# Attention on VectorE: both row statistics in the sixth step and the row moments in the eighth

## The chip, the cores and the metric

The kernel runs on one core of a Trainium2 chip. The metric is the time of one execution on the device in microseconds (us), smaller is better. Five engines work side by side from queues of their own: TensorE (PE, its weight loads are shown as PEld), VectorE (DVE), ScalarE (ACT), GpSimd (POOL) and SyncE (SP, which here only issues DMAs). They meet through semaphores alone. A name with a q behind it (DVEq, SPq) is the engine's own instruction queue.

## The reference, cut to what matters

An input of 32 x 375 x 256 is tokenised by a convolution of stride 2 to B = 32 batches of S = 188 rows of D = 256 columns, then comes an attention with 16 heads of 16 columns, then a mixture of 16 experts. The change lies in the attention stage and in what that stage prepares for the next layer norm.

```python
h = _L0_tok_ref(x, ...)
h = h + _L0_attn_ref(_layernorm(h, axis=-1), ...)
h = h + _L0_ffn_ref(_layernorm(h, axis=-1), ...)

# _L0_attn_ref
scores = jnp.einsum('bhqd,bhkd->bhqk', qh, k_rec) / math.sqrt(d)
scores = scores * decay[None, None, :, :]
attn = jax.nn.softmax(scores, axis=-1)
out = jnp.einsum('bhqk,bhkd->bhqd', attn, v_rec)
return out.transpose(0, 2, 1, 3).reshape(b, s, d) @ W_o

# _layernorm
m = jnp.mean(x, axis=axis, keepdims=True)
v = jnp.var(x, axis=axis, keepdims=True)
```

The mean and the variance of each row of h after the attention are what "row statistics" and "row moments" mean below: `bn_stats` makes six numbers of a row of 256, `bn_aggr` makes mean and variance of the six.

## The kernel before

The attention stage is a software pipeline written out by hand. Every engine runs its own function `batch(b, par)` for b from -3 to 33, in the same order, b = 2 to 27 of them in a loop whose body holds two batches (the even one, then the odd one), the others as straight code. A batch has eight steps, j = 0 to 7, one for each pair of heads. "Step 5" below is the step with j = 5, which is the sixth.

In a step PE makes the scores of a pair of heads that lies LEAD = 11 steps ahead (`scores`, L1395, into the banks `SB`), subtracts the row maxima from the previous step's turned scores (`take_max`, L1409), makes the turned scores of this step (`turned_scores`, L1420, into `TB`), in odd steps weighs the values (`weigh`, L1441), and then does one job of another batch: in step 0 it projects values (L1463), in step 1 it turns the normalised rows (L1482), in step 2 it makes the output projection of batch b - 2 (L1498), in steps 4 and 6 it projects queries and keys of batch b + 3 (L1452), in step 5 it turns the maxima (L1508).

DVE's two fixed tasks of a step are `row_max` (three custom instructions of line L1086, each with a read of its accumulator) and `times_decay` (L1094). They and PE form a tight loop:

- `scores` of a step waits for `row_max` of the step before (semaphore `scaled`), and `row_max` waits for the step's `scores`;
- `times_decay` of step j waits for `turned_scores` of step j, and `take_max` of step j, which PE does in its step j + 1, waits for `times_decay` (semaphore `multiplied`).

The queue of DVE is in order, so whatever stands between two `row_max` delays both. The other tasks of DVE stand behind `times_decay` of their step:

- `x_norm` (L1036, step 0) normalises the rows of batch b + 3;
- `add_out` (L1059) and `invert` (L1052), step 3, for batches b - 2 and b - 1: `invert` makes the reciprocals of the softmax sums;
- `row_stats` (L1065), `row_moments` (L1072), `keep_moments` (L1078), for batch b - 2. Each waits on `dve2` or `y_added` for what it reads. `keep_moments` copies the moments of `row_moments` to `MV`, and waits for them. Nothing reads `MV` of these batches before the attention stage has ended;
- `low_max` (L1044, step 6), for which PE's `weigh` of step 7 waits.

A second chain goes round through the other engines, and the change doesn't touch any instruction of it. SP's order in a batch is a fixed list of 24 or so DMA issues: the spread queries and keys of later batches (L456), the reciprocals to memory (L485, waits for `invert`), more keys (L456), the store of the queries' halves (L462), the reciprocals back as rows (L496), and the store of the keys' halves (L462, waits for POOL's low halves of the keys, L592). When the reciprocals have landed, POOL multiplies by them (`divide`, L614), makes the high half (L618) and, at the start of its next batch, the low half (L592). The output projection of batch b - 2 on PE in step 2 (L1498) waits for that low half (`otl_ready`):

```python
                    pe.wait_ge(otl_ready, b - 1)
```

Of the kernel before, what the change touches and what calls it, by code (L numbers as in the profile page):

```python
# [105 lines left out]
def build(nc, x_t, conv_w, conv_b, gamma, beta, wq, wk_t, wv_t, wo, w_down, w_up_k, w_up_v, gate, s_g, s_u, s_d,  # L106
# [7 lines left out]
    with ctx:  # L114
# [167 lines left out]
        def valid(b):  # L282

            return not isinstance(b, int) or 0 <= b < B
# [119 lines left out]
        def hold(eng):  # L404

            eng.sem_inc(passed, 1)
# [537 lines left out]
        def _(dve):  # L944
# [83 lines left out]
            def x_norm(c):  # L1028
                if not valid(c):
                    return  # L1030
                if not isinstance(c, int) or c >= 1:
                    dve.wait_ge(xt_done, c)
                hold(dve)
                for qt in range(2):
                    t = 2 * c + qt
                    last = nc.vector.tensor_scalar(XN[0:HT, qt * D:(qt + 1) * D], H[0:HT, t, :], MV[0:HT, t, 0:1],  # L1036
                                                   RSTD[0:HT, t, :], ALU.subtract, ALU.mult)
                last.then_inc(xn_ready, 1)

            def low_max(c, par):  # L1040
                if valid(c):
                    dve.wait_ge(mth_ready, 2 * c + 2)
                    for p in (0, 32):
                        last = nc.vector.scalar_tensor_tensor(MT[par][64 + p:64 + p + HP, :], MB[p:p + HP, 0:S], -1.0 / 16, MT[par][p:p + HP, :],  # L1044
                                                              ALU.mult, ALU.subtract)
                    last.then_inc(mt_ready, 1)

            def invert(c):
                if valid(c):
                    dve.wait_ge(sums_in, 16 * c + 16)  # L1050
                    at_least(dve, rs_out, 16 * c)
                    nc.vector.reciprocal(RS[0:64, :], SUMS[0:64, :]).then_inc(sums_inverse, 1)  # L1052

            def add_out(c):
                if valid(c):
                    dve.wait_ge(y_done, c + 1)
                    hold(dve)
                    both = H[0:HT, bass.ts(c, 2), :].rearrange("p t n -> p (t n)")
                    nc.vector.scalar_tensor_tensor(both, WB[0:HT, :], 1.0 / WSCALE, both, ALU.mult, ALU.add).then_inc(y_added, 1)  # L1059

            def row_stats(c, qt):
                if valid(c):
                    dve.wait_ge(y_added, c + 1)
                    hold(dve)
                    nc.vector.bn_stats(STAT2[qt][0:HT, :], H[0:HT, 2 * c + qt, :]).then_inc(dve2, 1)  # L1065

            def row_moments(c):
                if valid(c):
                    dve.wait_ge(dve2, 5 * c + 2)
                    hold(dve)  # L1070
                    for qt in range(2):
                        nc.vector.bn_aggr(AGGR2[0:HT, 2 * qt:2 * qt + 2], STAT2[qt][0:HT, :]).then_inc(dve2, 1)  # L1072

            def keep_moments(c):
                if valid(c):
                    dve.wait_ge(dve2, 5 * c + 4)
                    hold(dve)
                    nc.vector.tensor_copy(MV[0:HT, bass.ts(c, 2), :], hsplit(AGGR2[0:HT, :])).then_inc(dve2, 1)  # L1078

            def row_max(b, par, j):  # L1080
                c, cpar, i = ahead(b, par, j, LEAD)
                if valid(c):
                    dve.wait_ge(s_done, HP * c + i + 1)
                    hold(dve)
                    for t in range(3):
                        last = nc.vector.tensor_tensor_reduce(  # L1086
                            out=SC[t], in0=SB[t], in1=C[:, C_DECAY + t * S:C_DECAY + (t + 1) * S], scale=1.0, scalar=-3e38,
                            op0=ALU.mult, op1=ALU.max, accum_out=MAX[cpar][:, t * HP + i:t * HP + i + 1])
                    last.then_inc(scaled, 1)

            def times_decay(b, j):
                if valid(b):
                    dve.wait_ge(st_done, HP * b + j + 1)
                    nc.vector.tensor_tensor(TB[j % 2], TB[j % 2], C[:, C_DECAY:C_DECAY + 3 * S], ALU.mult).then_inc(multiplied, 1)  # L1094

            def batch(b, par):
                for j in range(HP):
                    row_max(b, par, j)
                    times_decay(b, j)
                    if j == 0:  # L1100
                        x_norm(b + 3)
                    elif j == 3:
                        add_out(b - 2)
                        invert(b - 1)
                    elif j == 4:
                        row_stats(b - 2, 0)
                    elif j == 5:
                        row_stats(b - 2, 1)
                    elif j == 6:
                        low_max(b + 1, 1 - par)  # L1110
                        row_moments(b - 2)
                    elif j == 7:
                        keep_moments(b - 2)

            batches(dve, batch)
            meet(dve)

# [648 lines left out]
```

## Time and profile before

| | |
|---|---|
| time before, median of 3 runs (lowest to highest) | 1870.95 us (1870.95 to 1874.34) |
| time of the profiled execution | 1870.4 us |
| its span, first to last instruction | 1868.6 us |
| attention stage | from about 150 us to 794 us of the span |
| a batch of the loop, undisturbed | 18.03 us (for one: DVE's L1094 of step 0 at 450.88 and at 468.91) |
| PE busy over the span | 1689.0 us, 90% |
| DVE busy over the span | 1224.8 us, 66% |
| POOL busy over the span | 950.2 us, 51% |

The profiled execution lies 1.8 us over its span, so what changes in the span changes in the time by as much. The columns of a timeline row are its start in us from the start of the span, its length in us, the engine, the source line, the operation, what it writes and reads, and in square brackets how long its engine stood idle before it and what ended the idle time. Rows of matmuls are merged, and their ends are modelled.

### The profile page before, as it was taken

The numbers are of one execution on the slowest core, as the hardware profiler recorded it, in microseconds if no ns is written. First come the engines' busy times: TensorE is split into PE (matmuls) and PEld (weight loads), VectorE is DVE, ScalarE is ACT, GpSimd is POOL, SyncE is SP. The second block draws the span as 40 slices with busy tenths as digits, with TensorE's granted clock in tenths as the row PEclk, the third lists the DMA queues.
The fourth block names the chain that finished last, engine by engine and source line by source line (L and its number), as shares of the span: only waits on it lengthen the run. The fifth ranks groups of instructions, "written<-read, shape, count | busy, mean of one in ns | idle before, by whom it ended". The sixth has DMA issues, their size and how long they took to land.

```text
span 1868.6 us, 46715 instructions
## 1 busy us (share of the span) xinstructions
PE 1689.0 (90%) x15566; PEld 1232.2 (66%) x15566; DVE 1224.8 (66%) x3739; ACT 902.6 (48%) x1965; POOL 950.2 (51%) x945
## 2 busy tenths in 40 slices
PE   6874899999999999579999669999999999999997
PEld 5873566666666665357777537777777777777775
DVE  3883788888888888384778655555555555555551
ACT  4442566666666665244233634444444444444442
POOL 3771244444444443272224054666666666666665
PEclk9995999999999999789999779999999999999999
DMA  5522455555555555242010232333333334333322
GB/s 189 176 94 50 106 121 126 134 123 133 132 127 128 129 136 116 50 133 51 26 34 26 96 123 86 102 101 97 93 93 100 98 100 101 101 101 99 101 34 28
DMA packets 220234, 186.52 MB, mean 100 GB/s; under 512 B 165625, under 2 KB 200953, under 8 KB 214009
## 3 DMA queue, kind: packets, MB, share of 16 engines
q1 hardware_dynamic: 193272, 141.11, 28.2%
q0 software_dynamic: 26880, 44.36, 11.5%
q8 instruction: 48, 0.79, 0.2%
q14 instruction: 34, 0.27, 0.0%
HBM read 134.49 MB, written 50.44 MB: 99 GB/s over the span
## 4 chain that ended last, share of the span: by engine, by line
PE 70%; DVE 12%; issue 8%; POOL 4%; SPq 2%; ACT 2%; DMA 2%; DVEq 1%; POOLq 0%; ACTq 0%
PE psum L1678 26%; PE psum L1695 13%; PE psum L1542 6%; PE psum L1560 4%; DVE arena L1086 4%; DVE psum L1094 3%; PE psum L1441 3%; PE psum L1498 2%; PE psum L1395 2%; PE psum L1409 2%; PE psum L1463 2%; PE psum L1420 2%; POOL hidden L570 2%; POOL arena L575 1%; PE psum L1508 1%
## 5 line engine op out<-in xcount | busy, mean ns | idle before, releaser
L1678 PE MATMUL psum<-arena,hidden 128*128 128x376 f16 x3072 | 493.1, 323 | 0.9 <-DVE arena L1320 0.9
L634 POOL TENSOR_TENSOR arena<-arena 128x376 f16<-128x376 f32 x320 | 317.4, 994 | 343.9 <-ACT arena L727 342.5
L1678 PEld LDWEIGHTS psum<-arena,hidden 128*128 128x128 f16 x3072 | 301.0, 98 | 188.9 <-issue 1.6
L727 ACT ACTIVATE arena<-arena 128x376 f16<-128x376 f32 (+5 forms) x610 | 287.3, 474 | 54.0 <-DVE arena L1250 43.1
L1086 DVE CUSTOM_DVE_ANT_0 arena<-psum,constants 128x188 f32<-128x188 f32 x768 | 228.0, 345 | 106.8 <-PE psum L1395 105.4
L727 ACT ACTIVATE arena<-psum 128x188 f32<-128x188 f32 (+7 forms) x457 | 168.1, 398 | 257.6 <-PE psum L1658 74.9
L926 ACT ACTIVATE arena<-psum 128x376 f32<-128x376 f32 x256 | 123.7, 483 | 342.2 <-PE psum L1678 342.2
L1330 DVE SCALAR_TENSOR_TENSOR arena<-psum,arena 128x376 f32<-128x376 f32 x256 | 140.8, 550 | 189.3 <-ACT arena L926 187.8
L1695 PE MATMUL psum<-hidden,arena 128*128 128x256 f16 (+1 forms) x2304 | 256.6, 273 | 0.0
L1695 PEld LDWEIGHTS psum<-hidden,arena 128*128 128x128 f16 (+1 forms) x2304 | 229.8, 103 | 21.8
L776 ACT ACTIVATE arena<-psum 128x564 f32<-128x564 f32 x256 | 164.0, 641 | 98.6 <-PE psum L1409 97.0
L1312 DVE SCALAR_TENSOR_TENSOR hidden<-arena,hidden 128x512 f16<-128x512 f32 x192 | 209.2, 1095 | 0.0
L592 POOL TENSOR_TENSOR arena<-arena 128x376 f16<-128x376 f32 x128 | 115.5, 902 | 171.9 <-ACT arena L727 166.0
L1094 DVE TENSOR_TENSOR psum<-psum,constants 128x564 f32<-128x564 f32 x256 | 191.1, 747 | 7.4 <-PE psum L1420 7.2
L679 POOL DMA_INDIRECT out<-hidden,arena x96 | 149.8, 1561 | 45.2 <-DVE hidden L1340 23.1
L1340 DVE TENSOR_SCALAR hidden<-psum,arena 128x256 f32<-128x256 f32 x96 | 46.3, 483 | 164.9 <-PE psum L1695 164.6
L1542 PE MATMUL psum<-arena,weights_hi 128*128 128x376 f16 x512 | 136.3, 327 | 1.2 <-DVE arena L1125 1.2
L1441 PE MATMUL psum<-arena 128*32 128x188 f32 (+1 forms) x2048 | 126.7, 336 | 4.6 <-ACT arena L776 0.8
L1409 PE MATMUL psum<-arena 128*128 128x188 f16 x768 | 106.3, 247 | 26.4 <-DVE psum L1094 20.4
L1395 PE MATMUL psum<-arena 96*128 96x188 f16 x768 | 108.6, 251 | 23.0 <-DVE arena L1086 13.2
L670 POOL DMA_INDIRECT arena<-token_table,arena x96 | 109.8, 1144 | 26.9 <-POOL arena L663 12.7
L727 ACT ACTIVATE hidden<-arena 128x512 f16<-128x512 f32 x192 | 117.9, 619 | 0.0
(156 smaller groups left out, 2644.2 us busy)
## 6 DMA issues: line engine op xcount, KB each, us to landing
arena<-q_halves SPq DMA_DIRECT2D x384, 47.0 KB, 2.4
arena<-k_halves SPq DMA_DIRECT2D x384, 47.0 KB, 2.3
arena<-e_g SPq DMA_DIRECT2D x16, 1024.0 KB, 5.1
arena<-e_u SPq DMA_DIRECT2D x16, 1024.0 KB, 5.2
arena<-e_d SPq DMA_DIRECT2D x16, 1024.0 KB
arena<-x_t SPq DMA_DIRECT2D x32, 376.0 KB, 3.5
weighed<-arena POOLq DMA_DIRECT2D x32, 376.0 KB, 3.9
q_halves<-arena SPq DMA_DIRECT2D x32, 188.0 KB, 3.1
```

The lines of the kernel that those rows point to most:

```text
L634: nc.gpsimd.tensor_tensor(dst, f, hi, ALU.subtract).then_inc(ready, 1)
L679: nc.gpsimd.indirect_dma_start(out[:, :], bass.IndirectOffsetOnAxis(ap=IDXS[par][0:n, m:m + 1], axis=0), EO[par][0:n, m * D:(m + 1) * D], ...
L727: return nc.scalar.activation(dst, src, ACT.Copy, scale=scale)
L776: nc.scalar.activation(PT[i % RING], TB[i % 2], ACT.Exp).then_inc(exp_done, 1)
L1086: last = nc.vector.tensor_tensor_reduce(out=SC[t], in0=SB[t], in1=C[:, C_DECAY + t * S:C_DECAY + (t + 1) * S], scale=1.0, scalar=-3e38, op ...
L1094: nc.vector.tensor_tensor(TB[j % 2], TB[j % 2], C[:, C_DECAY:C_DECAY + 3 * S], ALU.mult).then_inc(multiplied, 1)
L1312: nc.vector.scalar_tensor_tensor(WEL[par][:, c], WST[:, c], WSCALE, WEH[par][:, c], ALU.mult, ALU.subtract).then_inc(wl_ready[i], 1)
L1395: last = mm(SB[t], QD[cpar][0:2 * KR, i * CW + t * 128:i * CW + (t + 1) * 128], KX[cpar][0:2 * KR, i * S:(i + 1) * S], start=True, stop=True)
L1441: last = mm(OB[32 * k:32 * k + 32, :], V[cpar][p0:p0 + rows, v:v + 32], PT[a % RING][p0:p0 + rows, t * S:(t + 1) * S], start=n == 0, stop= ...
L1542: last = mm(bank[2 * (m % 2) + i][:, 0:CHUNK], w_, a, start=n == 0, stop=n == 5)
L1678: last = mm(bank[2 * (s % 2) + i][:, 0:CHUNK], w_, a, start=n == 0, stop=n == 5)
L1695: last = mm(bank[down_bank[m]][0:rows, 0:D], a, w_, start=n == 0, stop=n == 23)
```

## The change

Both `row_stats` calls of a batch move into step 5, behind its `times_decay`; before, one stood in step 4 and one in step 5. `row_moments` moves from step 6, where it stood behind `low_max`, to step 7, behind `times_decay` and directly ahead of `keep_moments`. `add_out` and `invert` stay in step 3. No instruction is added or taken away.

```diff
                     elif j == 3:
                         add_out(b - 2)
                         invert(b - 1)
-                    elif j == 4:
+                    elif j == 5:
                         row_stats(b - 2, 0)
-                    elif j == 5:
                         row_stats(b - 2, 1)
                     elif j == 6:
                         low_max(b + 1, 1 - par)
+                    elif j == 7:
                         row_moments(b - 2)
-                    elif j == 7:
                         keep_moments(b - 2)
```

In DVE's queue, in the even batch of the loop, the end of step 6 and the start of step 7 read before (L1044 is `low_max`, L1072 `row_moments`, L1086 the first instruction of `row_max` of step 7; ISA and REGISTER_ALU rows are semaphore and address work of the queue):

```order
L1044 SCALAR_TENSOR_TENSOR arena<-psum,arena 8x188
L1069 ISA
L1072 BN_AGGR arena<-arena 94x2 [waits dve2]
L1072 BN_AGGR arena<-arena 94x2
L1083 REGISTER_ALU
L1086 ISA arena<-psum,constants 128x188 [waits scores_done]
```

The end of step 7 and the start of step 0 of the next batch read before (L1094 is `times_decay` of step 7, L1078 `keep_moments`, L1086 `row_max` of step 0):

```order
L1093 REGISTER_ALU
L1094 TENSOR_TENSOR psum<-psum,constants 128x564 [waits turned_scores_done]
L1076 REGISTER_ALU
L1078 ISA [waits dve2]
L1078 COPY mean_var<-arena 94x4
L1083 REGISTER_ALU
L1086 ISA arena<-psum,constants 128x188 [waits scores_done]
```

The same place of the changed kernel, with the same names:

```order
L1093 REGISTER_ALU
L1094 TENSOR_TENSOR psum<-psum,constants 128x564 [waits turned_scores_done]
L1069 ISA
L1072 BN_AGGR arena<-arena 94x2 [waits dve2]
L1072 BN_AGGR arena<-arena 94x2
L1076 REGISTER_ALU
L1078 ISA [waits dve2]
L1078 COPY mean_var<-arena 94x4
L1083 REGISTER_ALU
L1086 ISA arena<-psum,constants 128x188 [waits scores_done]
```

The two aggregations have moved past a whole `row_max` and `times_decay`, and the copy, which waits for them, is now their direct neighbour in the queue.

In step 5 of the changed kernel DVE's queue reads, from `times_decay` of step 5 to `row_max` of step 6:

```order
L1094 TENSOR_TENSOR psum<-psum,constants 128x564 [waits turned_scores_done]
L1065 BN_STATS arena<-hidden 94x6 [waits y_added]
L1065 ISA [waits y_added]
L1065 BN_STATS arena<-hidden 94x6
L1083 REGISTER_ALU
L1086 ISA arena<-psum,constants 128x188 [waits scores_done]
```

The first L1065 stood one `row_max` and one `times_decay` further ahead before. The queues of ACT and SP and the work of PE and POOL are the same in both kernels.

## Rows read from the trace of the kernel before

**Rows 1.** First line of the page.

```profile
span 1868.6 us, 46715 instructions
```

**Rows 2.** Timeline of DVE, step 6 of batch 14 to step 1 of batch 15.

```profile
466.24 0.24 DVE L1072 BATCH_NORM_AGGREGATE arena<-arena 94x2 f32<-94x6 f32 x2
466.51 0.35 DVE L1086 CUSTOM_DVE_ANT_0 arena<-psum,constants 128x188 f32<-128x188 f32 x1
...
467.34 0.75 DVE L1094 TENSOR_TENSOR psum<-psum,constants 128x564 f32<-128x564 f32 x1
468.00 0.16 DVE L1078 COPY mean_var<-arena 94x4 f32 x1
468.09 0.35 DVE L1086 CUSTOM_DVE_ANT_0 arena<-psum,constants 128x188 f32<-128x188 f32 x1
...
468.91 0.75 DVE L1094 TENSOR_TENSOR psum<-psum,constants 128x564 f32<-128x564 f32 x1
469.57 0.72 DVE L1036 TENSOR_SCALAR arena<-hidden,mean_var,rstd 94x256 f32 x2
470.78 0.35 DVE L1086 CUSTOM_DVE_ANT_0 arena<-psum,constants 128x188 f32<-128x188 f32 x1 [0.49 <-PE psum L1395]
...
471.61 0.75 DVE L1094 TENSOR_TENSOR psum<-psum,constants 128x564 f32<-128x564 f32 x1
```

**Rows 3.** Timeline of PE, steps 0 and 2 of batch 15.

```profile
467.48 0.42 PE L1395 MATMUL psum<-arena 96*128 96x188 f16 x3 [0.19 <-DVE arena L1086]
468.15 0.42 PE L1409 MATMUL psum<-arena 128*128 128x188 f16 x3 [0.25 <-DVE psum L1094]
...
472.54 0.41 PE L1409 MATMUL psum<-arena 128*128 128x188 f16 x3
...
473.03 0.42 PE L1498 MATMUL psum<-weights_hi,arena 128*94 128x256 f16 x2
```

**Rows 4.** Timeline of DVE, end of step 5 and start of step 6, batch 14.

```profile
462.61 0.41 DVE L1065 BATCH_NORM_STATS2 arena<-hidden 94x6 f32 x1
463.89 0.35 DVE L1086 CUSTOM_DVE_ANT_0 arena<-psum,constants 128x188 f32<-128x188 f32 x1 [0.88 <-PE psum L1395]
```

**Rows 5.** Timeline of DVE in the convolution: a copy that waits for L970.

```profile
107.53 0.27 DVE L1000 COPY mean_var<-arena 94x8 f32 x1 [0.24 <-DVE arena L970]
```

**Rows 6.** Timeline of POOL, batch 15: divide, then low half.

```profile
470.19 0.99 POOL L614 TENSOR_TENSOR arena<-arena 128x376 f32<-128x376 f32 x1 [2.18 <-DMA arena<-inverse_sums]
...
471.95 0.90 POOL L592 TENSOR_TENSOR arena<-arena 128x376 f16<-128x376 f32 x1
```

**Rows 7.** Timeline, batches 7 and 27: low half and output projection.

```profile
327.20 0.90 POOL L592 TENSOR_TENSOR arena<-arena 128x376 f16<-128x376 f32 x1
...
328.25 0.41 PE L1498 MATMUL psum<-weights_hi,arena 128*94 128x256 f16 x2
...
688.97 0.90 POOL L592 TENSOR_TENSOR arena<-arena 128x376 f16<-128x376 f32 x1
...
690.09 0.42 PE L1498 MATMUL psum<-weights_hi,arena 128*94 128x256 f16 x2
```

**Rows 8.** Timeline of POOL and SP, end of batch 13.

```profile
449.07 0.90 POOL L592 TENSOR_TENSOR arena<-arena 128x376 f16<-128x376 f32 x1 [3.51 <-ACT arena L727]
...
450.13 0.41 SPq L462 DMA_DIRECT2D k_halves<-arena  x1
```

**Rows 9.** Timeline of DVE and POOL, step 0 of batch 14.

```profile
451.25 0.98 POOL L614 TENSOR_TENSOR arena<-arena 128x376 f32<-128x376 f32 x1 [1.28 <-DMA arena<-inverse_sums]
...
451.54 1.17 DVE L1036 TENSOR_SCALAR arena<-hidden,mean_var,rstd 94x256 f32 x2
```

**Rows 10.** Timeline of DVE and POOL, step 0 of batch 27.

```profile
686.63 0.72 DVE L1036 TENSOR_SCALAR arena<-hidden,mean_var,rstd 94x256 f32 x2
687.19 1.02 POOL L614 TENSOR_TENSOR arena<-arena 128x376 f32<-128x376 f32 x1 [2.13 <-DMA arena<-inverse_sums]
```

**Rows 11.** Timeline of POOL and DVE, step 7 of batch 30.

```profile
756.65 0.97 POOL L614 TENSOR_TENSOR arena<-arena 128x376 f32<-128x376 f32 x1 [6.59 <-DMA arena<-inverse_sums]
756.72 0.94 DVE L1078 COPY mean_var<-arena 94x4 f32<-94x4 f32 x1
```

## The prediction

> **What bounds the kernel now.** The change touches the attention stage alone, which is about a third of the span [rows 1], so I read DVE's timeline there first. The steady batches are alike to 0.01 us, and I take batch 15 as the example.
>
> In step 7 and step 0 DVE is never idle, and PE waits for it. The aggregations start at 466.24 and `row_max` of step 7 at 466.51; `times_decay` of step 7 starts at 467.34 and ends at 468.09, and PE's `take_max` starts at 468.15 after 0.25 us of idleness, as its `scores` did at 467.48 after 0.19 [rows 2, 3]. So 0.27 us of `row_moments` lie on the path between PE and DVE there. In step 1 it is the other way round: DVE idles 0.49 us until PE's scores are there [rows 2].
>
> Then I asked who else holds PE in a batch, and read POOL beside PE. In batch 15 POOL's low half of the attention output starts at 471.95, ends at 472.85, and PE's output projection, which waits for it, starts at 473.03, 0.18 later [rows 3, 6]. In batch 7 the distance is 328.25 - 328.10 = 0.15, in batch 27 it is 690.09 - 689.87 = 0.22; [rows 7]; these are the first and the last of the eleven odd batches 7 to 27, over which it is 0.14 to 0.22. The shortest, 0.14, must be what the release of PE takes. So in every second batch PE comes to its output projection less than 0.1 us after the half is there, and in six of the eleven exactly when it is: **two paths end together**.
>
> Where does that half come from? From the reciprocals' DMA, for which `divide` waited 2.18 us [rows 6]; that DMA is late because SP issues it as the last but one of its list, and SP began the list when the keys' halves of batch 13 were there: POOL's L592 at 449.07 to 449.97, SP's store at 450.13 [rows 8]. From there to `divide` are 470.19 - 450.13 = 20.06 us. The store is released by PE's key projection in step 6 of batch 13. So the loop is closed over two batches: key projection of batch 13, POOL, SP's list, DMA, `divide`, output projection in step 2 of batch 15, four steps of PE, key projection of batch 15. None of the moved instructions lies on it: steps 2 to 6 hold only the statistics, which I cost below at nothing. **This loop sets the pace of two batches; the path through step 7 and step 0 is as long as it to within 0.1 us.**
>
> **The change part by part.**
>
> *The first `row_stats` leaves step 4.* It frees 0.33 us on DVE ahead of `row_max` of step 5. PE doesn't wait for DVE in step 5 or at the start of 6: it weighs, turns the maxima, and then DVE waits for PE, 0.88 us [rows 4]. Gain 0. If PE did wait, 0.33 a batch.
>
> *It arrives in step 5*, where two statistics now end about 0.33 us later than the one did, inside those 0.88 us [rows 4]. Cost 0; without that cover 0.33 a batch, about 10 us in all.
>
> *`row_moments` leaves step 6.* `row_max` and `times_decay` of step 7 start 466.51 - 466.24 = 0.27 us sooner [rows 2], and with them `take_max` in PE's step 0. This is -0.27 a batch for the path of PE and DVE.
>
> *It arrives in step 7, with a copy right behind that waits for it.* Behind `times_decay` now come 0.24 us of aggregations, then the copy's own wait. The trace has that wait in the convolution, where a copy with address work in its queue stands 0.24 us idle behind the same operation [rows 5]. Before, the copy's moments were a step old and the copy started on the tick at 468.00 [rows 2]. The bounds are nothing and 0.24; I take 0.24, it is the same pair of operations. From `times_decay` of step 7 now starting at 467.07: aggregations at 467.73 to 467.97, copy at 468.21, `row_max` of step 0 at 468.3 to 468.4 instead of 468.09. So DVE is 0.2 to 0.3 us later in step 0 than before, while PE is 0.27 earlier. What hides it: PE doesn't need step 0 of DVE until `take_max` of step 1, behind the value projection, and in step 1 DVE had 0.49 us to spare [rows 2]. After: `times_decay` of step 0 at about 469.15, `x_norm` 469.8 to 470.55, scores there at 470.5. So the -0.27 survives to PE's step 1. If that cover were gone the step would be 0.25 a batch slower.
>
> The Trainium skill has a rule on this term: on the page "VectorE: DVE Perf Modes", section "The DRAIN you can't avoid", chained operations with a semaphore after each took as long as without, "the semaphore costs nothing extra here". By it the copy would start at 467.97 and DVE would be level with before. The trace doesn't agree, by 0.24 us [rows 5], and the sum goes by the trace; either way the sum is the same, since step 1 hides it.
>
> *`x_norm` against `divide`.* In even batches `divide` (451.25 to 452.23) lies on `x_norm`, which takes 1.17 instead of 0.72 us and ends 0.48 after it [rows 9]. There `x_norm` ends with `divide`, so a later start costs nothing, and PE, which has 0.12 us to spare behind `times_decay` of step 1 (472.54 against 472.36 + 0.06 [rows 2, 3]), gets at first only some 0.1 of its 0.27 us. As even batches get earlier, their `divide` does too.
>
> *What reaches the end.* In an odd batch PE arrives early at its output projection and waits for POOL. Of -0.27 a batch only the excess over 0.14 us is left: 0.01, 0, 0.04, 0, 0.04, 0, 0, 0, 0.08, 0, 0.08, together **0.25 us** for the eleven odd batches. Outside this regime a boundary between batches counts in full, if nothing else holds PE. I count one on the way in (batch 4 to 5) and two on the way out (27 to 28 and 29 to 30), 3 x 0.24 = **0.7 us** as an estimate from the 0.27. The boundary 30 to 31 gives nothing: the copy stands under `divide` there, 0.94 us long [rows 11], and will again. The last two batches have no `row_max`, and the chain of the reciprocals sets them.
>
> Sum: 0.25 + 0.7 = 0.95, so the profiled execution's 1870.4 becomes about 1869.5. The median of the runs is 0.55 above it, so I say 1870.0.
>
> **The rivals.**
>
> *The whole gain arrives (faster).* If PE's odd output projection isn't held by POOL, or POOL's chain gets shorter with PE, each of the 29 boundaries of batches 2 to 30 gives 0.27: 7.8 us, 1863. For it: PE's idle time is real [rows 3] and goes away. Against it: eleven times a distance within 0.08 us of the shortest isn't chance. Chance 0.12.
>
> *`divide` catches `x_norm` in odd batches too (slower).* Its two instructions, of 0.40 us each, take 0.72 together, so they start 0.32 us apart, and the second is caught if `divide` starts before it. `divide` starts 0.62 us behind `x_norm` in batch 15 and 0.56 in batch 27, the smallest; the largest is 1.00 [rows 2, 6, 10]. The margin is thus 0.24 to 0.68 us. A DVE that is 0.2 to 0.3 later in step 0 uses up the smallest, if the even batch gave nothing back; if it gave 0.27 back, as I expect once the pattern has settled, `x_norm` starts where it did. Price of a catch: `x_norm` ends at 471.18 + 0.47 = 471.65, `take_max` of step 1 can start at 473.29 instead of 472.54, so 0.75 us for an odd batch. Five catches are 3.7 us and eleven 8.3; the point from which it decides is a shift of some 0.3 us. I put it at +5, 1876. The Trainium skill, "SBUF — State Buffer", section "SBUF: two separate sides", says that VectorE and GpSimd take a shared port in turn for a whole instruction, "the other fully blocks"; the trace agrees, with 1.17 us and 0.94 us [rows 9, 11]. Chance 0.08.
>
> *The same, but by drift.* DMAs land at other times and the loop over two batches takes 0.1 us more or less each time; 11 x 0.2 = 2.2 us either way. This is inside the forecast.
>
> **How the numbers follow.** A measurement of this kernel can tell about 0.2%, 3.7 us, from no change. No change that shows: 0.80, faster 0.12, slower 0.08. The likeliest case has its own range 1867 to 1874 (the sum, the drift of 2.2, and the highest of the runs shown, 1874.34). With the outer cases let in by half the range is 1864 to 1875.
>
> **What would show it.** In the changed profile, from `times_decay` of step 7 to that of step 0 about 2.1 us instead of 468.91 - 467.34 = 1.57, and `row_max` of step 7 right behind `low_max`, where L1072 stood; a copy with about 0.24 us of idle time behind L1072; PE waiting for POOL's L592 ahead of L1498 in all odd batches by 0.2 to 0.5 us; two batches still 36.1 us. Wrong would be: two batches at 35.6 or less (the first rival), or `x_norm` above 1 us in odd batches (the second). What I can't see is whether the wait of the copy also holds the queue's later address work, so that DVE falls back further than 0.3 us.

## The result, and the profile after

The changed kernel takes 1877.02 us (median of 22 runs, 1872.74 to 1882.10) against 1873.89 us before (22 runs, 1870.95 to 1879.71): 3.1 us more. The ratio is 1.0019 with a 95% interval of 1.0012 to 1.0027. I had forecast no change at 1870.0 us. Of the 7.0 us between that and the result 2.9 are the median of the kernel before, which was 1870.95 over the three runs shown and 1873.89 over 22; 3.1 are the kernel; the rest is the 0.95 us of gain that I had summed up and that did not come.

The profiled execution has a span of 1872.7 us against 1868.6 [rows 1]. Head of its page:

```profile
span 1872.7 us, 46715 instructions
PE 1690.0 (90%) x15566; PEld 1230.2 (66%) x15566; DVE 1235.2 (66%) x3739; ACT 904.4 (48%) x1965; POOL 946.8 (51%) x945
```

The same number of instructions, and DVE is busy 10.4 us longer (1235.2 against 1224.8). Most of it has nothing to do with the change: 6.6 us belong to the 192 instructions of one line of the experts' stage (L1312 before, L1311 now, 210.1 against 216.8 us). The two instructions of `x_norm` (L1036) take 34.5 us in all instead of 32.4. The sum hides what matters below: over the batches 8 to 27, `x_norm` became shorter in the even batches (1.26 to 0.85 us on average) and longer in the odd ones (0.72 to 1.22 us).

As a measure that the scatter of single runs at the start and the end of the stage doesn't touch, I use the time of two batches, from the start of DVE's `times_decay` in step 0 of batch 8 to that in step 0 of batch 28, divided by ten. Before: (704.01 - 342.16) / 10 = 36.18 us. After: (709.83 - 343.58) / 10 = 36.63 us. That is 0.44 us for two batches, 5.7 us if all thirteen pairs of the loop lose as much. From batch 28 to batch 31 the changed kernel was 1.5 us faster (704.01 to 757.57 before and 709.83 to 761.84 now), but over the traces of this document this stretch takes anything from 52.0 to 56.9 us, so that is not shown to be an effect of the change. The measure comes from one trace of each kernel. The kernel before, the same without `x_norm` and the one with the statistics alone give 36.18, 36.18 and 36.30 us below, so differences of about 0.1 us mean nothing.

First the boundary between steps 7 and 0 in DVE's timeline, at the end of batch 13, which is the last batch of the loop's body (it answers to [rows 2]):

```profile
451.30 0.75 DVE L1094 TENSOR_TENSOR psum<-psum,constants 128x564 f32<-128x564 f32 x1
451.95 0.23 DVE L1072 BATCH_NORM_AGGREGATE arena<-arena 94x2 f32<-94x6 f32 x2
452.44 0.17 DVE L1078 COPY mean_var<-arena 94x4 f32 x1 [0.26 <-DVE arena L1072]
453.10 0.35 DVE L1086 CUSTOM_DVE_ANT_0 arena<-psum,constants 128x188 f32<-128x188 f32 x1 [0.49 <-issue]
...
453.93 0.75 DVE L1094 TENSOR_TENSOR psum<-psum,constants 128x564 f32<-128x564 f32 x1
```

and at the end of batch 14, in the middle of the loop's body:

```profile
469.42 0.75 DVE L1094 TENSOR_TENSOR psum<-psum,constants 128x564 f32<-128x564 f32 x1
470.08 0.23 DVE L1072 BATCH_NORM_AGGREGATE arena<-arena 94x2 f32<-94x6 f32 x2
470.56 0.17 DVE L1078 COPY mean_var<-arena 94x4 f32 x1 [0.25 <-DVE arena L1072]
470.82 0.35 DVE L1086 CUSTOM_DVE_ANT_0 arena<-psum,constants 128x188 f32<-128x188 f32 x1
...
471.65 0.75 DVE L1094 TENSOR_TENSOR psum<-psum,constants 128x564 f32<-128x564 f32 x1
```

The copy waits 0.25 us for its neighbours in both, as forecast. But then `row_max` of step 0 doesn't follow it in 0.09 us as before. At the end of batch 14 it starts 0.26 us behind the copy's start, at the end of batch 13 it starts 0.66 us behind, of which 0.49 are idle time that no other engine causes. From `times_decay` of step 7 to that of step 0 these are 2.23 and 2.63 us, where it was 1.57 in every batch; the two lengths alternate through the whole loop. The trace's records of the queue itself show what stands in the longer one: behind the copy, the compare and branch of the loop (L299) and a register instruction of the same line.

The last batches are straight code, without a branch and without addresses to work out. There the same place, at the end of batch 28, reads:

```profile
725.56 0.75 DVE L1094 TENSOR_TENSOR psum<-psum,constants 128x564 f32<-128x564 f32 x1
726.22 0.23 DVE L1072 BATCH_NORM_AGGREGATE arena<-arena 94x2 f32<-94x6 f32 x2
726.60 0.17 DVE L1078 COPY mean_var<-arena 94x4 f32<-94x4 f32 x1
726.78 0.35 DVE L1086 CUSTOM_DVE_ANT_0 arena<-psum,constants 128x188 f32<-128x188 f32 x1
727.61 0.75 DVE L1094 TENSOR_TENSOR psum<-psum,constants 128x564 f32<-128x564 f32 x1
```

The copy follows the aggregations after about 0.15 us instead of 0.25, `row_max` follows the copy after 0.18, and from `times_decay` to `times_decay` it is 2.05 us. So the neighbourhood alone costs 0.48 us (2.05 instead of 1.57), the address work 0.18 more, and the branch 0.40 more.

What that does in step 1 of the even batch, in PE's timeline (`take_max` in PE's steps 0 and 1, and the output projection, now L1497; it answers to [rows 3]):

```profile
452.10 0.42 PE L1408 MATMUL psum<-arena 128*128 128x188 f16 x3 [0.23 <-DVE psum L1094]
...
454.74 0.42 PE L1408 MATMUL psum<-arena 128*128 128x188 f16 x3 [0.20 <-DVE psum L1094]
...
457.35 0.42 PE L1497 MATMUL psum<-weights_hi,arena 128*94 128x256 f16 x2
```

The second wait, of PE for `times_decay` of step 0, did not exist before; it stands in each of the even batches 8 to 26. And in an odd batch, here batch 17, DVE first and then POOL and PE:

```profile
508.19 0.75 DVE L1094 TENSOR_TENSOR psum<-psum,constants 128x564 f32<-128x564 f32 x1
508.85 1.54 DVE L1036 TENSOR_SCALAR arena<-hidden,mean_var,rstd 94x256 f32 x2
510.31 0.34 DVE L1086 CUSTOM_DVE_ANT_0 arena<-psum,constants 128x188 f32<-128x188 f32 x1
...
509.24 1.00 POOL L614 TENSOR_TENSOR arena<-arena 128x376 f32<-128x376 f32 x1 [2.34 <-DMA arena<-inverse_sums]
...
511.26 0.42 PE L1394 MATMUL psum<-arena 96*128 96x188 f16 x3 [0.18 <-DVE arena L1086]
511.93 0.41 PE L1408 MATMUL psum<-arena 128*128 128x188 f16 x3 [0.25 <-DVE psum L1094]
```

`divide` started 0.39 us behind `x_norm` instead of 0.56 or more, and `x_norm` took 1.54 us instead of 0.72. `row_max` of step 1 followed at once, and PE waited for both tasks of it. Of the ten odd batches 9 to 27 seven have such an `x_norm`, of 1.36 to 1.54 us, and in all seven PE waits for `times_decay` of step 1. In five of them `divide` starts behind `x_norm`, in two (11 and 21) up to 0.10 us ahead of it. The other three (9, 15, 23) have `x_norm` at 0.72 us and wait for POOL's low half, 0.43 to 0.95 us. In batch 15 `divide` was just too late to stretch `x_norm`, and became longer itself:

```profile
472.31 0.72 DVE L1036 TENSOR_SCALAR arena<-hidden,mean_var,rstd 94x256 f32 x2
472.72 1.17 POOL L614 TENSOR_TENSOR arena<-arena 128x376 f32<-128x376 f32 x1 [2.36 <-DMA arena<-inverse_sums]
```

Measured on PE, from `turned_scores` of step 0 to that of the next batch, an even batch takes 18.22 us on average instead of 18.03, and an odd one 18.44 instead of 18.15.

Step 5 is as forecast (it answers to [rows 4]):

```profile
464.73 0.74 DVE L1065 BATCH_NORM_STATS2 arena<-hidden 94x6 f32 x2
466.25 0.35 DVE L1086 CUSTOM_DVE_ANT_0 arena<-psum,constants 128x188 f32<-128x188 f32 x1 [0.79 <-PE psum L1394]
```

DVE still waits 0.79 us for PE behind the two statistics.

### The profile page after: what moved, and what is told of

Its sections match the earlier page's. It is cut to its first block, busy times and chain, and to the rows that moved or that the text cites. A ratio compares the mean times of both kernels' runs of the same rounds, so it can differ in the third digit from the quotient of the medians.

```text
span 1872.7 us, 46715 instructions
## 1 busy us (share of the span) xinstructions
PE 1690.0 (90%) x15566; PEld 1230.2 (66%) x15566; DVE 1235.2 (66%) x3739; ACT 904.4 (48%) x1965; POOL 946.8 (51%) x945
## 4 chain that ended last, share of the span: by engine, by line
PE 63%; DVE 12%; issue 9%; POOL 6%; SPq 3%; DMA 3%; ACT 2%; DVEq 1%; POOLq 0%; ACTq 0%
PE psum L1677 26%; PE psum L1694 13%; PE psum L1541 6%; DVE arena L1086 4%; PE psum L1559 4%; DVE psum L1094 4%; SPq L456 2%; PE psum L1497 2%; PE psum L1440 2%; POOL hidden L570 2%; PE psum L1408 1%; POOL arena L575 1%; PE psum L1394 1%; DMA arena<-inverse_sums 1%; PE psum L1657 1%
## 5 line engine op out<-in xcount | busy, mean ns | idle before, releaser
L1086 DVE CUSTOM_DVE_ANT_0 arena<-psum,constants 128x188 f32<-128x188 f32 x768 | 228.4, 346 | 101.7 <-PE psum L1394 93.0
L1311 DVE SCALAR_TENSOR_TENSOR hidden<-arena,hidden 128x512 f16<-128x512 f32 x192 | 215.9, 1129 | 0.0
L592 POOL TENSOR_TENSOR arena<-arena 128x376 f16<-128x376 f32 x128 | 115.2, 900 | 180.4 <-ACT arena L727 175.0
L1094 DVE TENSOR_TENSOR psum<-psum,constants 128x564 f32<-128x564 f32 x256 | 191.2, 747 | 7.0 <-PE psum L1419 6.8
```

What stands on the lines that cost most here:

```text
L1086: last = nc.vector.tensor_tensor_reduce(out=SC[t], in0=SB[t], in1=C[:, C_DECAY + t * S:C_DECAY + (t + 1) * S], scale=1.0, scalar=-3e38, op ...
L1311: nc.vector.scalar_tensor_tensor(WEL[par][:, c], WST[:, c], WSCALE, WEH[par][:, c], ALU.mult, ALU.subtract).then_inc(wl_ready[i], 1)
```

## The experiments

My theory after the result, A, says that the loss is the wait of the copy for its direct neighbours in DVE's queue. It costs its own 0.25 us and also uncovers what the queue would else have done under running work: the work on addresses (0.17 us more) and at the end of the loop's body the branch (another 0.4). DVE is then 0.4 and 0.8 us behind in step 0, which is more than the room that it had there. The rivals: B, the second statistic in step 5; C, the loop's branch alone; D, the place of the aggregations in step 7 as such; and, from the prediction, whether POOL's chain really is a second path of the same length.

Each ratio is taken against runs of the kernel before that were made together with those of the row.

| kernel | two batches, us | start of step 0's L1094 (L1095), batch 8, batch 28 | ratio to before, 95% interval |
|---|---|---|---|
| before | 36.18 | 342.16, 704.01 | |
| after | 36.63 | 343.58, 709.83 | 1.0019 (1.0012 to 1.0027) |
| statistics alone | 36.30 | 343.79, 706.82 | 1.0003 (0.9991 to 1.0016) |
| aggregations alone | 36.82 | 346.71, 714.95 | 1.0025 (1.0014 to 1.0036) |
| aggregations moved in even batches | 36.54 | 340.31, 705.75 | 1.0012 (1.0000 to 1.0024) |
| aggregations moved in odd batches | 36.52 | 348.45, 713.63 | 1.0015 (1.0004 to 1.0026) |
| aggregations ahead of step 7's `times_decay` | 36.10 | 343.41, 704.37 | 0.9988 (0.9976 to 1.0000) |
| aggregations and copy in step 5 | 35.90 | 340.83, 699.86 | 0.9977 (0.9967 to 0.9987) |
| the same, both statistics in step 4 | 35.84 | 341.59, 700.01 | 0.9975 (0.9963 to 0.9986) |
| after, no `x_norm` in the loop | 36.06 | 342.39, 702.96 | one run |
| before, no `x_norm` in the loop | 36.18 | 342.22, 704.04 | one run |
| before, chain longer | 37.11 | 344.47, 715.55 | 1.0058 (1.0041 to 1.0074) |
| after, chain longer | 37.01 | 344.21, 714.31 | 1.0051 (1.0033 to 1.0069) |
| statistics in 4, rest in 5, chain longer | 36.76 | 343.64, 711.20 | 1.0057 (1.0040 to 1.0073) |

**The statistics alone.**

```diff
-                    elif j == 4:
-                        row_stats(b - 2, 0)
                     elif j == 5:
+                        row_stats(b - 2, 0)
                         row_stats(b - 2, 1)
```

> Only the two statistics are moved to step 5; the aggregations stay in step 6. Theory A (the copy's own wait behind the aggregations in step 7 costs the time): no change, ratio 1.000 within 0.001, two batches of the loop 36.1 to 36.3 us as before, from times_decay of step 4 to that of step 5 about 1.57 us and from step 5 to step 6 about 3.0. Theory B (the second statistic in step 5 comes too late for step 6): as slow as the full change, 36.6 us for two batches.

Measured: 36.30 us, 1.0003. From `times_decay` of step 4 to step 5 it is 1.56 to 1.57 us in every batch, and 3.0 from step 5 to step 6. The 0.12 us above the kernel before are within what single traces differ by. B falls: the statistics cost nothing that can be measured.

**The aggregations alone.**

```diff
                         low_max(b + 1, 1 - par)
-                        row_moments(b - 2)
                     elif j == 7:
+                        row_moments(b - 2)
                         keep_moments(b - 2)
```

> Only the aggregations are moved, to step 7; the statistics stay in steps 4 and 5. Theory A: the whole loss, ratio 1.0015 to 1.003, two batches 36.6 us, from times_decay of step 7 to that of step 0 2.23 us after an even batch and 2.64 after an odd one. Theory B: as before, 36.2 us.

Measured: 36.82 us, 1.0025: the whole loss, with 2.23 and 2.63 us from step 7 to step 0. It is 0.2 us above the changed kernel in this one trace. There in four even batches (8, 12, 18 and 26) `x_norm` takes 1.62 to 1.69 us although `divide` had ended by then: it runs together with the two operations that follow on POOL, the high half (L618) and the low half (L592).

**In even batches or in odd batches alone.** The kernel for even batches; the other has the two conditions exchanged. Both have the statistics in step 5.

```diff
                     elif j == 6:
                         low_max(b + 1, 1 - par)
+                        if par == 1:
+                            row_moments(b - 2)
                     elif j == 7:
+                        if par == 0:
+                            row_moments(b - 2)
                         keep_moments(b - 2)
```

> Both statistics in step 5; the aggregations move to step 7 in even batches alone, so that their copy's wait never stands ahead of the loop's branch. Theory A: 2.23 us from step 7 to step 0 after even batches, 1.57 after odd ones; the odd batch's x_norm is 0.4 us later and meets the divide, while even batches are as before: two batches 36.2 to 36.5 us, ratio 1.000 to 1.0015. If the branch alone mattered (theory C), it would be at or below before, 36.1.

> The aggregations move to step 7 in odd batches alone, the last of the loop's body. Theory A: 2.64 us from step 7 to step 0 after odd batches, PE waits 0.2 us for times_decay in step 1 of even batches, which gain nothing or lose 0.1 to 0.2 us; odd batches as before, held by POOL's chain: two batches 36.2 to 36.4 us. Theory C (the exposed branch is the whole loss): 36.6 us, ratio 1.002.

Measured: 36.54 and 36.52 us, both slower, both with the boundaries as expected (2.23 and 1.57; 1.57 and 2.63). C falls in its strong form, since the kernel without any uncovered branch is slower too, by 0.36 us for two batches; its ratio alone, 1.0012 with an interval down to 1.0000, would not say it clearly. Both lie above what I expected of A (36.2 to 36.5 and 36.2 to 36.4), and the second taken by itself fits C better. Each half alone costs more than half, so the two effects don't add up. A doesn't explain this: in the kernel for even batches six of the ten odd batches (9, 11, 15, 17, 19, 21) have `x_norm` at 0.72 us, and PE waits 0.42 to 1.48 us for POOL there. From the end of SP's last read issue to `divide` it is 3.13 us on average instead of 2.87. Why the reads land later was not settled. In the kernel for even batches the copy of batch 14, which waits for its neighbours, and that of batch 15, whose aggregations are a step old, stand in DVE's timeline like this:

```profile
467.90 0.17 DVE L1078 COPY mean_var<-arena 94x4 f32 x1 [0.25 <-DVE arena L1072]
468.16 0.35 DVE L1086 CUSTOM_DVE_ANT_0 arena<-psum,constants 128x188 f32<-128x188 f32 x1
...
485.99 0.15 DVE L1078 COPY mean_var<-arena 94x4 f32 x1
486.08 0.35 DVE L1086 CUSTOM_DVE_ANT_0 arena<-psum,constants 128x188 f32<-128x188 f32 x1
```

The second is at the loop's branch, and yet `row_max` follows in 0.09 us: the branch costs nothing where the queue has run ahead.

**The aggregations ahead of `times_decay` in step 7.** All else as in the changed kernel.

```diff
                     row_max(b, par, j)
+                    if j == 7:
+                        row_moments(b - 2)
                     times_decay(b, j)
...
                     elif j == 7:
-                        row_moments(b - 2)
                         keep_moments(b - 2)
```

> As the full change, but the aggregations of step 7 stand ahead of that step's times_decay instead of behind it, so that 0.65 us of other work lie between them and the copy that waits for them. Theory A (the wait of a neighbour, which also holds the queue's later work, is the loss): back to before, from times_decay of step 7 to that of step 0 1.57 us, two batches 36.1 to 36.3 us, ratio 1.000. Theory D (any place of the aggregations in step 7 is too late for step 0): 36.6 us, ratio 1.002.

Measured: 36.10 us, 0.9988, with 1.53 us from step 7 to step 0 behind even batches and 1.82 behind odd ones, where I expected 1.57 behind both. The loss is gone with the neighbourhood; D falls. At the end of batch 15, the last of the loop's body, DVE's timeline is:

```profile
486.09 0.72 DVE L1094 TENSOR_TENSOR psum<-psum,constants 128x564 f32<-128x564 f32 x1
486.73 0.16 DVE L1078 COPY mean_var<-arena 94x4 f32 x1
487.09 0.35 DVE L1086 CUSTOM_DVE_ANT_0 arena<-psum,constants 128x188 f32<-128x188 f32 x1 [0.20 <-issue]
```

The copy starts without idle time. The branch shows a little, 0.20 us: the copy's wait is over only 0.1 us behind the start of `times_decay`, and the queue reaches the branch 0.4 us behind it. In the kernel before, the branch was done before `times_decay` of step 7 started.

**Aggregations and copy in step 5**, where VectorE stood idle 0.88 us [rows 4]; in the second kernel both statistics stand in step 4.

```diff
                     elif j == 5:
                         row_stats(b - 2, 1)
+                        row_moments(b - 2)
+                        keep_moments(b - 2)
                     elif j == 6:
                         low_max(b + 1, 1 - par)
-                        row_moments(b - 2)
-                    elif j == 7:
-                        keep_moments(b - 2)
```

> Statistics in steps 4 and 5 as before, and the aggregations and the copy right behind them in step 5, where VectorE was idle 0.88 us. Steps 6 and 7 lose the 0.27 us of the aggregations and the 0.09 of the copy. The copy's wait is the same as in the changed kernel, but under cover. Theory A with two paths of one length (POOL's chain holds every odd batch): two batches 36.0 to 36.2 us, ratio 0.999 to 1.000, PE waits for POOL ahead of the output projection in all odd batches. Rival (no chain): 0.3 us less for each batch, 35.5 us for two, ratio 0.995.

> Both statistics in step 4, aggregations and copy in step 5: as the kernel with all in step 5, but with 0.33 us more of cover in step 5 and 0.33 us less in step 4. Theory A with two paths: 36.0 to 36.2 us, ratio 0.999 to 1.000, the same as that kernel within 0.001.

Measured: 35.90 and 35.84 us, 0.9977 and 0.9975, some 4 us less than before. These beat both kernels. The copy has the same wait, under cover, here in batch 15 of the second kernel:

```profile
479.56 0.23 DVE L1072 BATCH_NORM_AGGREGATE arena<-arena 94x2 f32<-94x6 f32 x2
480.05 0.17 DVE L1078 COPY mean_var<-arena 94x4 f32 x1 [0.26 <-DVE arena L1072]
480.53 0.35 DVE L1086 CUSTOM_DVE_ANT_0 arena<-psum,constants 128x188 f32<-128x188 f32 x1 [0.31 <-PE psum L1394]
```

0.31 us of idle time for PE are left behind the copy. Both gained more than I expected of A with two equal paths (36.0 to 36.2) and far less than the rival's 35.5. Where the gain goes is seen in batch 15 of the second kernel, POOL's low half and PE's output projection:

```profile
470.62 0.90 POOL L592 TENSOR_TENSOR arena<-arena 128x376 f16<-128x376 f32 x1
...
471.67 0.39 PE L1497 MATMUL psum<-weights_hi,arena 128*94 128x256 f16 x2 [0.23 <-POOL arena L592]
```

A batch in which nothing holds PE is 17.75 us there instead of 18.03, which is the 0.28 in full. Nine of the ten even batches 8 to 26 take 17.75 to 17.77 us, and all odd batches give some of it back, 0.04 to 0.57 us. Two batches could be 35.50, and are 35.84.

**Without `x_norm` in the loop**, once in the changed kernel and once in the one before. The two instructions of the normalisation of rows are left out in the loop's batches, and the attention works on old rows there.

```diff
                     if j == 0:
-                        x_norm(b + 3)
+                        if isinstance(b, int):
+                            x_norm(b + 3)
+                        else:
+                            dve.wait_ge(xt_done, b + 3)
+                            hold(dve)
+                            dve.sem_inc(xn_ready, 1)
```

> The changed kernel without the normalisation of rows (x_norm) in the loop's batches: the two instructions are left out, the attention works on old rows there. Theory A with collisions (VectorE, 0.4 and 0.8 us late, has no room left in step 0 because of x_norm and of the divide that holds it up): the loss goes, two batches 36.0 to 36.3 us. If POOL's chain alone had grown longer: 36.5 us or more as in the changed kernel.

> The kernel before without the normalisation of rows (x_norm) in the loop's batches, left out in the same way as in the run before. Theory A: the kernel before had room in step 0, so two batches stay at 36.0 to 36.2 us and equal the 36.06 us of the changed kernel without it within 0.15. If x_norm cost time in both kernels alike, this one would be 0.4 us below that, 35.6.

Measured: 36.06 and 36.18 us. The kernel before doesn't notice, the changed one loses its loss. The same boundary as above, in the changed kernel without `x_norm`:

```profile
485.39 0.17 DVE L1078 COPY mean_var<-arena 94x4 f32 x1 [0.26 <-DVE arena L1072]
486.05 0.35 DVE L1086 CUSTOM_DVE_ANT_0 arena<-psum,constants 128x188 f32<-128x188 f32 x1 [0.49 <-issue]
...
486.88 0.75 DVE L1094 TENSOR_TENSOR psum<-psum,constants 128x564 f32<-128x564 f32 x1
487.67 0.35 DVE L1086 CUSTOM_DVE_ANT_0 arena<-psum,constants 128x188 f32<-128x188 f32 x1
```

The late start is all there, and PE still waits 0.2 us for `times_decay` of step 0 in even batches; together this costs two batches nothing when step 0 has room. The edit takes away the time that `x_norm` needs by itself and its stretch by POOL together. The changed kernel's own trace tells them apart: PE's step 1 takes 2.12 us in the three odd batches in which `x_norm` takes 0.72 us, as before, and 2.71 to 2.89 us in the seven in which it is stretched. So it is the stretch that costs.

**POOL's chain made longer.** One of the four reads of the reciprocals is cut in two: the same bytes in five issues. The core of the edit, made to the kernel before, the changed one, and the one with both statistics in step 4:

```diff
-                    for g in range(4):
-                        sp.dma_start(RD[64 * (g % 2):64 * (g % 2) + 64, g // 2 * S:(g // 2 + 1) * S],
-                                     heads[g].unsqueeze(1).broadcast_to((4, HD, S))).then_inc(rd_in, 16)
+                    for g, r0, r1 in ((0, 0, 2), (0, 2, 4), (1, 0, 4), (2, 0, 4), (3, 0, 4)):
+                        p0 = 64 * (g % 2) + HD * r0
+                        sp.dma_start(RD[p0:p0 + HD * (r1 - r0), g // 2 * S:(g // 2 + 1) * S],
+                                     heads[g][r0:r1].unsqueeze(1).broadcast_to((r1 - r0, HD, S))).then_inc(rd_in, 16)
...
-                    pool.wait_ge(rd_in, 64 * c + 64)
+                    pool.wait_ge(rd_in, 80 * c + 80)
```

> The kernel before with POOL's chain made longer: one of the four reads of the reciprocals is cut in two, the same bytes in five issues of some 0.55 us. Theory of two paths of nearly one length: the chain holds PE in odd batches 0.4 us more, two batches 36.5 to 36.8 us, ratio 1.002 to 1.004. Rival (the chain has room): 36.2 us, ratio 1.000.

> The changed kernel with the same five issues. If VectorE is now the longer path in most pairs of batches, the longer chain costs less than before: two batches 36.7 to 36.9 us against 36.63. If the chain sets it here too: 37.1 us.

> Both statistics in step 4, aggregations and copy in step 5, with the same five issues. There the chain holds PE in nearly all odd batches, so the whole 0.55 us shows: two batches 36.35 to 36.5 us against 35.84. Rival: below 36.1.

Measured: 37.11, 37.01 and 36.76 us, so +0.92 for the kernel before, +0.39 for the changed one, +0.92 for the third. The size was off, the chain became 0.9 us longer and not 0.55. SP's own rows show why, the reads of one batch in the kernel before and in the same kernel with five issues:

```profile
465.20 2.24 SPq L496 DMA_DIRECT2D arena<-inverse_sums  x4
...
470.00 3.09 SPq L497 DMA_DIRECT2D arena<-inverse_sums  x5
```

The five issues take 0.85 us longer than the four, in every batch: the two halves take 0.69 and 0.62 us, where the whole took 0.56. From the last issue to `divide` it is as long as before (2.96 us on average against 2.87). The pattern is the expected one: the chain sets the time in the kernel before and in the one with both statistics in step 4, and less than half of the delay shows in the changed kernel, where VectorE had become the longer path. With the longer chain the changed kernel is no slower than the one before (37.01 against 37.11). PE's output projection in two odd batches of the kernel before with five issues:

```profile
553.01 0.39 PE L1499 MATMUL psum<-weights_hi,arena 128*94 128x256 f16 x2 [1.23 <-POOL arena L593]
590.17 0.39 PE L1499 MATMUL psum<-weights_hi,arena 128*94 128x256 f16 x2 [0.96 <-POOL arena L593]
```

## Why the prediction was wrong

*Right: the statistics cost nothing.* Step 5 and the kernel with the statistics alone show it.

*Right: -0.27 for the path through step 7.* `row_max` of step 7 follows `low_max` at once, and in the kernels with all in step 5 a free batch is 17.75 us, 0.28 less.

*Wrong, the step that failed: "It arrives in step 7, with a copy right behind that waits for it", its term "DVE is 0.2 to 0.3 us later in step 0".* The wait itself is 0.25 us, as I took it. I left out what stands behind a wait in a queue. `row_max` came 0.26 and 0.66 us behind the copy's start instead of the 0.1 to 0.2 that I allowed. From `times_decay` of step 6 to that of step 0 DVE needs 4.57 and 4.98 us where it was 4.19: it is 0.38 and 0.8 us later, not 0.2 to 0.3. I had named this as the thing I couldn't see, and gave it no price and no place in the range. The 0.24 us that I took for the wait from the convolution was right for the loop, but it holds some address work too: in straight code the copy waits only about 0.15.

*Wrong with it: "so the -0.27 survives to PE's step 1".* The cover of 0.49 us in step 1 has to pay for the lateness of DVE and for the 0.27 us by which PE comes earlier. With my 0.24 this was 0.51, with nothing left; measured it is 0.65 in odd batches and 1.07 in even ones. In even batches PE now waits for `times_decay` of step 0, and its step 0 takes 2.63 us instead of 2.27, so the 0.27 is gone before step 1. I also counted from batch 15 alone. "The steady batches are alike to 0.01 us" holds for the even batches, 18.03 us; the odd ones took 18.03 to 18.38.

*The rival "`divide` catches `x_norm` in odd batches too" came true, with seven of ten odd batches, for 1.36 to 1.54 us each.* I had priced a catch at 0.75 us for PE and the point from which it decides at a shift of 0.3 us. The shift was there, and PE's step 1 became 0.6 to 0.8 us longer in these batches, close to the price. But the odd batch also gains the boundary's 0.27 and wasn't free of POOL's wait before, so the even and the odd batch together lose 0.44 us, and the sum for the whole kernel, +5, was too high by 2. Two readings behind the price were wrong. I had the second instruction of `x_norm` caught only if `divide` starts before it, 0.32 us behind `x_norm`. In all traces of this document taken together, each of the 50 `divide` that start up to 0.39 us behind `x_norm` stretches it, and none that starts 0.40 us behind it or later does. And `x_norm` then ends 0.15 us behind `divide`; it ends 0.47 behind only where `divide` starts less than 0.09 us behind `x_norm`. I gave it 0.08, because I expected that the even batches would give 0.27 back and keep `x_norm` where it was; they gave nothing back, since their own start was 0.8 late. The Trainium skill's sentence that one of the two engines "fully blocks" on the shared port ("SBUF — State Buffer", section "SBUF: two separate sides") agrees with the trace in both directions: in batch 17 of the changed kernel `divide` held up `x_norm`, 1.54 us instead of 0.72, and in batch 15 `divide` began under `x_norm` and took 1.17 us instead of 0.99. That is 0.18 us more, though `x_norm` had 0.31 us to go.

*Half right: two paths of one length.* The experiments with a longer chain show that POOL's chain sets the pace of the kernel before. But it is not fixed: when PE's path gets 0.56 us shorter for two batches, the chain lets 0.34 of it through. The traces say where. Averages in us over the odd batches 9 to 27:

| part of the chain | before | after | both statistics in step 4, rest in 5 |
|---|---|---|---|
| SP's store of the keys' halves at the end of an odd batch to `divide` in the next odd one | 20.20 | 20.35 | 19.88 |
| `divide` to the output projection | 2.83 | 3.18 | 2.80 |
| that output projection to the next such store | 13.16 | 13.13 | 13.16 |

In the changed kernel 0.35 of the loss lies between `divide` and the output projection, where POOL's half is ready and PE comes late, and 0.15 in front of `divide`. In the faster kernel SP's 31 issues of a batch (not some 24, as I had said) take 17.10 us instead of 17.32, nearly all of it in one read of queries (0.33 instead of 0.52 us), and the reads of the reciprocals land 0.08 earlier. Why that one issue is shorter was not settled. From SP's last issue to `divide` it is 2.70 to 3.15 us in the kernel before, from batch to batch.

*The tail.* In batch 30 the copy, 0.94 us long under `divide` before [rows 11], is 0.17 us long and isn't caught any more. I had written that it would be again. My 0.7 us for the batches outside the regime can't be checked: single traces of this stretch differ by more.

*The time itself.* The median of three runs stood 2.9 us under that of 22. I took it as the base, and let the range end 0.7 us above the highest of the three runs. From the base that I took, the loss of 3.1 us would have ended at 1874.1, inside the range. The mechanism failed apart from that: I forecast a gain of 0.95 us, and it is a loss of 3.1.

## What to carry to other kernels

In this kernel an instruction that waits for its direct neighbour on the same engine cost more than the wait: nothing behind it in the queue was prepared, so address work and above all the loop's branch came out from under the work that had hidden them. Keep one other task between a producer and its consumer on an in-order engine (with 0.65 us of other work the copy had no wait here), or put the pair where the engine waits for another one anyway; the latter turned 0.2% of loss into 0.2% of gain with the same instructions. And count a cover for every kind of iteration, against the lateness of the one engine and the earliness of the other together: here even and odd batches differ in what hides them.

## What the runs showed of the hardware

- A DVE copy that waits on a semaphore of the aggregation right in front of it starts 0.25 us after its end in the loop and about 0.15 us after it in straight code. The next instruction starts 0.18 us (straight code), 0.26 us (address work between) or 0.66 us (the loop's branch between) after the copy's start. Without the wait it is 0.09 us, and the branch costs nothing.
- Two float32 `tensor_scalar` instructions of 0.40 us on DVE and a float32 `tensor_tensor` of 0.99 us on POOL hold each other up. If POOL's starts up to 0.39 us behind the first of DVE's, DVE's pair takes 1.39 to 1.55 us instead of 0.72 and ends 0.15 us behind POOL's (0.47 us if POOL's starts less than 0.09 us behind it). If POOL's starts 0.40 us behind it, DVE's pair keeps its 0.72 us and POOL's takes 1.17 us.
- Four DMA issues on SP that read the reciprocals take 2.24 us. The same bytes in five, one of the four cut in two, take 3.09 us, and two batches of the kernel before take 0.92 us more.
